# Attention and mixture-of-experts kernel: places of their own for the copies out of PSUM, LayerNorm factors on GpSimd, a mean-free Wo, and one maximum over two PSUM banks

## The chip, the cores and the metric

The kernel is written by hand in Bass and runs on one core of a Trainium2 chip. The metric is the device time of one execution in microseconds; lower is better. The five engines of the core run their own instruction lists in order and meet through semaphores: PE (TensorE), DVE (VectorE), ACT (ScalarE), POOL (GpSimd) and SP (SyncE, which here only issues transfers).

## The reference

Two sandwich blocks over 8 sequences of 256 tokens with 256 features. The first is grouped-query attention with 32 query heads and 8 key heads of size 8, the second a mixture of experts with two shared experts.

```
x = x + layernorm(attn(layernorm(x)) @ Wo + b_out)
x = x + layernorm(moe(layernorm(x)))
attn: q, k rotated by position; softmax(q k / sqrt(8)), causal; times v
moe:  scores = sigmoid(x @ w_router); the two best of 8 experts, weights normalised
      each expert: wd (silu(wg x) * (wu x)), inner size 640
      plus two shared experts of the same form for every token
layernorm(y) = (y - mean(y)) / sqrt(var(y) + 1e-5), no learned factors
```

## The kernel before

The 2048 tokens are 16 tiles of 128 rows. One function, `plan()`, writes a single list of stages, and each engine walks through the list and emits its own part of each stage, so the list is the order of every engine. The attention goes in 64 passes: pass n is one key head of one sequence (8 passes for each of the 8 sequences, two tiles each). `plan()` calls `step(n)` for each pass, and `step` goes through the string `ORDER`, whose letters are places within a step: `2` is `pass2` (scores in banks 0 to 2, `exp` on ACT, the causal mask on POOL), `a` and `b` are `early` and `late` (the scores of pass n+7 in other banks, of which DVE takes the row maxima; `tops` adds the last part of an early bank from within `pass2`), `w` is `weigh` (probabilities times values, two passes later), `v` is `back` (transposing the result, after which DVE divides), `m0` to `m3` are the four parts of `neg` (which splits the negated maxima of four passes into three bf16 terms), and `t` is `turn` (PE transposes them, ACT copies them into `NMT`, SP sends them with six transfers into rows 48 to 50 of the queries `QT`, where the next group's `pass2` needs them).

`s0` to `s3` are the four places of a step in which the work on the tiles stands: the tables `FRONT` and `BACK` give each stage a time in quarter steps, relative to the tile's sequence. The front of a tile is its first LayerNorm (`f_stats`, `f_dev`, `f_norm`), a transpose, the q, k, v product, the rotation with a three-way bf16 split of q and k (`f_rope`, `f_first`, `f_second`, `f_third`) and their transposes (`q0`, `q1`, `k`). The back is the product with Wo (`b_out`), its LayerNorm (`b_stats`, `b_dev`, `b_norm`), the sum with x (`b_add`), the second LayerNorm (`b_stats2`, `b_dev2`, `b_norm2`), a transpose into `XH` and `XL` (the fp32 value as a rounded part and a rest) and the router product (`b_route`).

In all of these one stage means the PE work and at the same place in the list the copy out of PSUM. Four PSUM banks, 3 to 6, go round among all stages but `pass2` and `weigh`, in turn, by `banks()`.

After pass 63 come 155 chunks c of expert work (`up`, `hh`, `hl`, `down`): 20 for the first shared expert, 115 for 23 blocks of 256 rows that the router chose, and 20 for the other shared expert. The backs of the last tiles are mixed into the first chunks, with two steps in each of chunks 0 to 13. The routing (`pick`, `rank`, `choose`, `token`) runs beside chunks 4 to 18; `xt` transposes the gathered rows of a block, and chunk 20 is the first that needs them. The weights of an expert are split into `WH` and `WL` by `split`.

Of the kernel before, what the change touches and what calls it, by code (L numbers as in the profile page):

```python
# [13 lines left out]
P = 128  # L14
# [22 lines left out]
FRONT = [("f_stats", -101), ("f_dev", -97), ("f_norm", -90), ("f_turn", -85), ("f_qkv", -77), ("f_rope", -77),  # L37
         ("f_first", -69), ("f_second", -67), ("f_third", -65), ("q0", -53), ("q1", -56), ("k", -49)]
BACK = [("b_turn", 47), ("b_out", 51), ("b_stats", 51), ("b_dev", 51), ("b_norm", 56), ("b_add", 59),
        ("b_stats2", 59), ("b_dev2", 59), ("b_norm2", 66), ("b_turn2", 71), ("b_route", 75)]  # L40
ORDER = "a 2 s0 d s1 b s2 v m0 t w m1 m2 m3 s3"
# [14 lines left out]
def plan():  # L56
# [5 lines left out]
    halves, turns, pairs = [], [], []  # L62

    def sides(n):
        for b in range(NB):
            for stages, lag in ((FRONT, LAG), (BACK, 16)):
                for what, at in stages:
                    for T in range(2):
                        if n == max(32 * b + at + lag * T, 4 * START):
                            out.append((what, 2 * b + T))  # L70

    def step(n):
        firsts = ahead.get(n, [])
        for o in ORDER.split():
            if o == "2" and 0 <= n < 64:
                out.append(("pass2", n))
            if o == "a":
# [24 lines left out]
            if o == "t":  # L102
                out.extend(("turn", m) for m in turns)
                turns.clear()
            if o[0] == "s":
                sides(4 * n + int(o[1]))

    for n in range(START, JOIN):
        step(n)
        if n == 0:  # L110
            out.append(("router_split", 0))
# [3 lines left out]
    for c in range(NC + 4):  # L115
        if c < 14:
            for n in (JOIN + 2 * c, JOIN + 2 * c + 1):
# [19 lines left out]
        if c == DENSE - 1:  # L137
# [1202 lines left out]
```

## Time and profile before

| | us |
|---|---|
| median of 3 runs | 758.98 (756.83 to 760.82) |
| the profiled execution | 760.28, span 757.8 from the first to the last instruction |
| PE busy | 705.5 (93%) |
| DVE busy | 605.7 (80%) |
| ACT busy | 431.8 (57%) |
| POOL busy | 314.7 (42%) |

The span has three parts: the attention, up to about 298 us; the first shared expert with the routing beside it, up to about 402 us; and the routed blocks and the second shared expert. A busy share is an average over all of them, so each part is read by itself. The ends of matmuls are modelled in such a profile, and a PE that is shown busy is not PE at its peak.

### The profile page before, as it was taken

What the parts mean: (1) busy time and instruction counts of PE and PEld (TensorE: products, weight loads), DVE (VectorE), ACT (ScalarE), POOL (GpSimd) and SP (SyncE); (2) the same over time, 40 slices, a digit from 0 to 9 for tenths busy, and PEclk for the clock granted to TensorE, in tenths of its full rate; (3) what the DMA queues carried; (4) which work ended last, traced back from release to release, by engine and by line L of the source; (5) the groups of instructions that cost most, each with busy time, mean ns of one, the idle gap of its engine ahead of it and who ended that gap; (6) DMA issues with size and microseconds to landing.
All of it is one profiled execution on the core that took longest, in us unless ns stands there. A gap on an engine that the chain in (4) does not pass through costs nothing. (4 is left out here: it accounts for less than half of the span.)

```text
span 757.8 us, 15818 instructions
## 1 busy us (share of the span) xinstructions
PE 705.5 (93%) x6002; PEld 564.7 (75%) x6002; DVE 605.7 (80%) x1364; ACT 431.8 (57%) x729; POOL 314.7 (42%) x444
## 2 busy tenths in 40 slices
PE   4779999999999998979998999999999999999994
PEld 2335555555555555768888999999999999988884
DVE  4998999999998885565866888888878878738885
ACT  2436765666667576334244777777776777632230
POOL 4113354454444455100223455445445543048854
PEclk9989999999999999989999999999999999999998
DMA  8000000000000000000124676776667676513311
GB/s 278 1 3 4 4 3 10 16 10 11 10 11 10 16 11 15 15 8 1 43 91 174 208 236 217 223 236 216 239 217 233 221 215 202 163 56 90 91 57 55
DMA packets 29131, 74.31 MB, mean 98 GB/s; under 512 B 4609, under 2 KB 18305, under 8 KB 29057
## 3 DMA queue, kind: packets, MB, share of 16 engines
q0 software_dynamic: 12208, 55.45, 22.6%
q1 hardware_dynamic: 16432, 17.20, 6.9%
q8 instruction: 48, 0.79, 0.4%
q10 hardware_dynamic: 416, 0.66, 0.3%
q14 instruction: 27, 0.21, 0.1%
HBM read 62.68 MB, written 10.22 MB: 96 GB/s over the span
## 5 line engine op out<-in xcount | busy, mean ns | idle before, releaser
L984 DVE TENSOR_TENSOR HF<-SS,PS 128x256 f32<-128x256 f32 (+1 forms) x155 | 75.9, 490 | 98.2 <-ACT SS L732 57.0
L732 ACT ACTIVATE SS<-PS 128x256 f32<-128x256 f32 (+1 forms) x155 | 68.2, 440 | 116.7 <-PE PS L396 112.2
L396 PE MATMUL PS<-XGH,WH 128*128 128x256 f32 x460 | 129.6, 282 | 2.8 <-DVE WL L1084 2.8
L396 PE MATMUL PS<-XGL,WH 128*128 128x256 f32 x460 | 129.3, 281 | 0.0
L396 PE MATMUL PS<-XGH,WL 128*128 128x256 f32 x460 | 129.3, 281 | 0.0
L821 DVE TENSOR_REDUCE NM<-PS 128x2 f32<-128x512 f32 (+1 forms) x192 | 122.6, 682 | 7.6 <-PE PS L396 6.6
L1084 DVE TENSOR_TENSOR WL<-RAW,WH 128x768 fp32r<-128x768 f32 x125 | 120.2, 963 | 3.5 <-ACT WH L659 2.8
L396 PE MATMUL PS<-WH,HH 128*128 128x256 f32 x390 | 112.4, 288 | 0.9 <-DVE ACC L995 0.8
L659 ACT ACTIVATE HH<-HF 128x256 fp32r<-128x256 f32 (+1 forms) x155 | 72.1, 465 | 71.4 <-DVE HF L984 64.1
L396 PE MATMUL PS<-WL,HH 128*128 128x256 f32 x390 | 110.4, 283 | 0.0
L396 PE MATMUL PS<-WH,HL 128*128 128x256 f32 x390 | 110.4, 283 | 0.0
L694 ACT ACTIVATE PF<-PS 128x1536 f32<-128x1536 f32 x64 | 92.9, 1451 | 27.4 <-PE PS L396 27.4
L1180 POOL TENSOR_SCALAR_AFFINE_SELECT PF<-PF 128x512 f32<-128x512 f32 x128 | 80.6, 654 | 62.9 <-ACT PF L694 62.9
L659 ACT ACTIVATE WH<-RAW 128x768 fp32r<-128x768 f32 x125 | 104.5, 838 | 1.0 <-DMA RAW<-in_wb,WIDX 0.7
L396 PEld LDWEIGHTS PS<-XGH,WH 128*128 128x128 f32 x460 | 86.7, 189 | 3.0 <-DVE WL L1084 3.0
L396 PEld LDWEIGHTS PS<-XGH,WL 128*128 128x128 f32 x460 | 87.3, 190 | 0.0
L396 PEld LDWEIGHTS PS<-XGL,WH 128*128 128x128 f32 x460 | 87.0, 189 | 0.0
L396 PEld LDWEIGHTS PS<-WH,HH 128*128 128x128 f32 x390 | 74.2, 190 | 3.3 <-issue 1.5
L1094 DVE TENSOR_TENSOR HL<-HF,HH 128x256 fp32r<-128x256 f32 (+1 forms) x155 | 76.4, 493 | 0.1
L396 PEld LDWEIGHTS PS<-WL,HH 128*128 128x128 f32 x390 | 74.5, 191 | 1.6
L1145 POOL TENSOR_SCALAR VE<-MV 128x1 f32<-128x1 f32 x64 | 19.0, 297 | 134.0 <-DVE MV L1020 46.8
L396 PEld LDWEIGHTS PS<-WH,HL 128*128 128x128 f32 x390 | 74.2, 190 | 0.0
(167 smaller groups left out, 1460.2 us busy)
## 6 DMA issues: line engine op xcount, KB each, us to landing
ys<-YO SPq DMA_DIRECT2D x23, 256.0 KB
RAW<-in_wsh SPq DMA_DIRECT2D x4, 768.0 KB, 6.5
X<-in_x SPq DMA_DIRECT2D x8, 256.0 KB, 5.3
xn<-YY SPq DMA_DIRECT2D x16, 128.0 KB, 1.7
out<-X SPq DMA_DIRECT2D x16, 128.0 KB
QT<-NMT SPq DMA_DIRECT2D x96, 4.0 KB
RAW<-in_wsh SPq DMA_DIRECT2D x2, 384.0 KB, 6.1
XG<-xn,XIDX POOLq DMA_INDIRECT x46
```

Source lines behind the costliest of these rows:

```text
L396: return eng.matmul(o, l, r, start=start, stop=stop, skip_group_check=True)
L659: return eng.activation(o, i, ACT.Copy)
L694: eng.activation(PF[:, i % 3, :], PS[:, 0:1536], ACT.Exp, scale=SCALE).then_inc(expd, 1)
L732: t = eng.activation(SS[:, i % 2, 0:n], bank(b, 0, n), ACT.Silu)
L821: eng.tensor_reduce(o, i, AXX, ALU.max, negate=True).then_inc(free[c], 1)
L984: eng.tensor_tensor(HF[:, c % 2, 0:n], SS[:, c % 2, 0:n], bank(b, 512 - n, 512) if n == 256 else bank(b), ALU.mult).then_inc(free[b], 1)
L1084: eng.tensor_tensor(WL[q % 2][:, c], RAW[:, c], WH[q % 2][:, c].bitcast(F32), ALU.subtract).then_inc(w_lo, 1)
L1094: eng.tensor_tensor(HL[:, i % 4, 0:n], HF[:, i % 2, 0:n], HH[:, i % 4, 0:n].bitcast(F32), ALU.subtract).then_inc(h_lo, 1)
L1145: eng.tensor_scalar(VE[:, i:i + 1], MV[:, i, 1:2], EPS, None, ALU.add, ALU.bypass).then_inc(ve, 1)
L1180: eng.affine_select(out=o, in_=o, pattern=[[0, 4], [1, 128]], base=0, channel_multiplier=-1, compare_op=ALU.is_ge, fill=0.0).then_inc(zero ...
```

## The change

Six things change.

1. Each copy out of PSUM becomes a stage of its own (`f_turned`, `f_taken`, `q0_out`, `b_taken`, `b_high`, `b_kept`, `divide`, `weighed`, `turned`, `exp`, and so on) with a place of its own in `ORDER` or in the tables. All tables get new numbers, with own tables for the first two sequences. `banks()` takes the bank that was used longest ago instead of strict turns.
2. The two maxima of a `late` pair are one DVE instruction over two neighbouring banks (`maxima`), and DVE frees both banks together.
3. `f_norm` and `b_norm2` move from DVE to POOL.
4. Wo and b_out have their row means subtracted at the start (`prepare`, on DVE in steps 1 to 6), so that the product has mean zero: `b_norm` is gone, and `b_add` multiplies by the factor and adds x in one instruction. The bias goes into PSUM through one more bf16 matmul, and ACT copies the sum out (`b_taken`) where DVE added the bias.
5. The router product takes both parts of its weights at once: 4 matmuls of 16 columns for 8 of 8, and DVE adds the two halves for all tiles (`pick` 0).
6. The copies of k in `KC` come out of wider casts: DVE has 4 instructions for 6 there.

```diff
-ORDER = "a 2 s0 d s1 b s2 v m0 t w m1 m2 m3 s3"
+ORDER = "a 2 b s0 d x l s1 m0 s2 v V w t T W m1 m3 s3 m2"
+RANK, TOKEN, ROWS0 = 11, 18, 19.0
...
+                    mm(bank(c, 0, 256), ones3[:, :], B3[:, :], True, False)
                     for k in range(2):
-                        t = mm(bank(c, 0, 256), CTT[:, i % 2, 128 * k:128 * k + 128], WO[:, k, :], k == 0, k == 1)
+                        t = mm(bank(c, 0, 256), CTT[:, i % 2, 128 * k:128 * k + 128], WO[:, k, :], False, k == 1)
...
-                        for a, r in ((XH, WRH), (XH, WRL), (XL, WRH), (XL, WRL)):
-                            t = mm(bank(c, 0, 8), a[:, k, 128 * i:128 * i + 128], r[:, 8 * k:8 * k + 8], n == 0, n == 7)
+                        for a in (XH, XL):
+                            t = mm(bank(c, 0, 16), a[:, k, 128 * i:128 * i + 128], WRX[:, k, :, :].rearrange("p a e -> p (a e)"),
+                                   k == 0 and a is XH, k == 1 and a is XL)
...
+                elif what == "b_taken":
+                    made(e, ("b_out", i))
+                    made(e, ("b_turn2", i - 2))
+                    e.wait_ge(d_xn[i % 2], 16 * (i // 2))
+                    copy(YY[:, i % 2, :], bank(c, 0, 256)).then_inc(free[c], 1)
...
-                eng.tensor_copy(K[:, :, 0:4:3, :], R[:, 32:40, :].unsqueeze(2).broadcast_to([P, 8, 2, 8]))
-                eng.tensor_copy(K[:, :, 5, :], R[:, 32:40, :]).then_inc(k_1, 1)
+                eng.tensor_copy(K[:, :, :, 1:6:2, :], R[:, 32:40, :].unsqueeze(2).unsqueeze(3).broadcast_to([P, 8, 2, 3, 8])).then_inc(k_1, 1)
...
-                eng.tensor_copy(KC[:, T, :, 1, :], KC[:, T, :, 0, :]).then_inc(k_5, 1)
...
+                    c = lates[k][0]
+                    e.wait_ge(laid, 2 * k + 2)
+                    eng.tensor_reduce(o.rearrange("p (j a) -> p a j", a=2), bank(c, 0, 1024).rearrange("p (a j t) -> p a j t", a=2, j=2),
+                                      AXX, ALU.max, negate=True).then_inc(n_m, 1)
...
+            def prepare(k):
+                if k < 3:
+                    e.wait_ge(d_bo if k == 2 else d_wo, 16)
+                    src = BO if k == 2 else WO[:, k, :]
+                    eng.bn_stats(BN[:, 48 + k, :], src[:, :]).then_inc(wo_s, 1)
...
-                    eng.tensor_tensor(YY[:, i % 2, :], bank(c, 0, 256), BO[:, :], ALU.add).then_inc(free[c], 1)
...
-                    normed(YY[:, i % 2, :], YY[:, i % 2, :], 16 + i).then_inc(b_yn, 1)
...
-                    eng.tensor_tensor(X1[:, i, :], X1[:, i, :], YY[:, i % 2, :], ALU.add).then_inc(b_x1, 1)
+                    e.wait_ge(b_rs, i + 1)
+                    eng.scalar_tensor_tensor(out=X1[:, i, :], in0=YY[:, i % 2, :], scalar=RS[:, 16 + i:17 + i], in1=X1[:, i, :],
+                                             op0=ALU.mult, op1=ALU.add).then_inc(b_x1, 1)
...
+                elif what == "b_norm2":
+                    e.wait_ge(c_rs, i + 1)
+                    made(e, ("b_turn2", i - 2))
+                    eng.tensor_scalar(YY[:, i % 2, :], X1[:, i, :], MV[:, 32 + i, 0:1], RS[:, 32 + i:33 + i],
+                                      ALU.subtract, ALU.mult).then_inc(c_x2, 1)
```

How the order moves, at three places. The first is DVE in the middle of the attention, where `b_out`, `b_stats` and `b_dev` of a tile meet the four parts of `neg`. `NM`, `NBF` and `NR` are the maxima and their bf16 terms, `BN` and `MV` the statistics, `YY` the product with Wo, `RA` and `RB` parts of the rotation. Before:

```order
L763 TENSOR_SCALAR YY<-X,MV,RS 128x256 [waits c_rs]
L850 RECIPROCAL RC<-PS 128x16 [waits free4,full4]
L853 TENSOR_TENSOR CTX<-PS,RC 128x2x64 [waits sums]
L833 CAST NBF<-NM 128x4x8 [waits free5,free6,free4,free3]
L836 TENSOR_TENSOR NR<-NM,NBF 128x32 [waits n_0]
L839 CAST NBF<-NR 128x4x8 [waits n_1]
L842 TENSOR_TENSOR NBF<-NR,NBF 128x4x8 [waits n_2]
L1047 TENSOR_TENSOR YY<-PS,BO 128x256 [waits d_xn1,full5]
L1050 BN_STATS BN<-YY 128x6 [waits free5]
L1053 BN_AGGR MV<-BN 128x2 [waits b_st]
```

And of the change:

```order
L892 CAST NBF<-NR 128x4x8 [waits n_1]
L827 TENSOR_TENSOR RA<-RQ,ROPE 128x320 [waits free6]
L828 TENSOR_TENSOR RB<-RQ,ROPE 128x40x4
L829 TENSOR_TENSOR RB<-RQ,ROPE 128x40x4
L870 TENSOR_REDUCE NM<-PS 128x4 [waits full4]
L874 TENSOR_REDUCE NM<-PS 128x2x2 [waits laid]
L1123 BN_STATS BN<-YY 128x6 [waits free3]
L895 TENSOR_TENSOR NBF<-NR,NBF 128x4x8 [waits n_2]
L1126 BN_AGGR MV<-BN 128x2 [waits b_st]
L1140 TENSOR_TENSOR XL<-PS,XH 128x2x128 [waits c_xh]
```

Two DVE instructions on `YY` are gone, steps that wait for each other no longer follow each other directly, and the last part of `neg` stands one step later.

The second place is ACT between the copy of `turn` into `NMT` and the `exp` of the first pass that needs it. `PF` is the output of an `exp`, one for each pass. Before, from the row behind the copy:

```order
L659 ACTIVATE NMT<-PS 48x256 [waits d_nm3,d_nm2,d_nm4,d_nm1,d_nm5,d_nm0,full6]
L659 ACTIVATE YC<-PS 128x256 [waits pv]
L659 ACTIVATE XH<-PS 128x2x128 [waits full3]
L694 ACTIVATE PF<-PS 128x1536 [waits scored]
L659 ACTIVATE QT<-PS 128x8x128 [waits full5]
L659 ACTIVATE ES<-PS 128x8 [waits full5]
L659 ACTIVATE QT<-PS 128x8x128 [waits full6]
L659 ACTIVATE XNT<-PS 128x256 [waits full3]
L694 ACTIVATE PF<-PS 128x1536 [waits pv,scored]
L659 ACTIVATE YC<-PS 128x256 [waits full4,pv]
L659 ACTIVATE CTT<-PS 128x256 [waits full3]
L659 ACTIVATE KT<-PS 128x8x128 [waits full4]
```

The row that follows is the `exp` that needs the transfers. Of the change:

```order
L744 ACTIVATE PF<-PS 128x1536 [waits scored]
L707 ACTIVATE QT<-PS 128x8x128 [waits full5]
L707 ACTIVATE NMT<-PS 48x256 [waits d_nm3,d_nm2,d_nm4,d_nm1,d_nm5,d_nm0,full3]
L707 ACTIVATE EW<-PS 128x16 [waits full4]
L707 ACTIVATE XNT<-PS 128x256 [waits full5]
L744 ACTIVATE PF<-PS 128x1536 [waits pv,scored]
L707 ACTIVATE CTT<-PS 128x256 [waits full5]
L707 ACTIVATE YC<-PS 128x256 [waits pv]
L707 ACTIVATE KT<-PS 128x8x128 [waits full6]
L744 ACTIVATE PF<-PS 128x1536 [waits scored]
```

One whole `exp` lies between the copy and the one that needs it, where there were two.

The third place is DVE at chunks 18 to 20, where the routed blocks begin. `XGL` is the rest part of the first block's rows, `WL` that of its weights. Before:

```order
L1084 TENSOR_TENSOR WL<-RAW,WH 128x768 [waits w_hi] x2
L968 TENSOR_REDUCE WAB<-EQ 128x16 [waits rt]
L969 TENSOR_TENSOR CMB<-CMB,EQ 128x128
L971 TENSOR_REDUCE WAB<-CMB 128x16 [waits rt]
L984 TENSOR_TENSOR HF<-SS,PS 128x512 [waits h_lo,full3,free2]
L1094 TENSOR_TENSOR HL<-HF,HH 128x512 [waits h_hi]
L1084 TENSOR_TENSOR WL<-RAW,WH 128x768 [waits w_hi] x3
L1098 TENSOR_TENSOR XGL<-PS,XGH 128x512 [waits x_hi]
```

And of the change:

```order
L1148 TENSOR_TENSOR WL<-RAW,WH 128x768 [waits w_hi] x2
L1052 TENSOR_REDUCE WAB<-EQ 128x16 [waits rt]
L1053 TENSOR_TENSOR CMB<-CMB,EQ 128x128
L1055 TENSOR_REDUCE WAB<-CMB 128x16 [waits rt]
L1162 TENSOR_TENSOR XGL<-PS,XGH 128x512 [waits x_hi]
L1068 TENSOR_TENSOR HF<-SS,PS 128x512 [waits h_lo,full3,free2]
L1158 TENSOR_TENSOR HL<-HF,HH 128x512 [waits h_hi]
L1148 TENSOR_TENSOR WL<-RAW,WH 128x768 [waits w_hi] x3
```

`XGL` moved ahead of chunk 19's work and of the three weight splits. `token` stands one chunk later on PE (before `up` 18 instead of before `up` 17), and `xt` 0 one chunk earlier (before `up` 19).

## Rows read from the trace of the kernel before

**Rows 1.** Busy time by stretch: from:to length, PE, PEld, DVE, ACT, POOL, clock, DMA.

```profile
60.00:80.00 20.00, 19.62 (x230) 10.90 (x224) 18.37 (x51) 14.60 (x18) 7.17 (x14) 0.97 0.02 4
154.49:188.84 34.35, 32.73 (x355) 19.24 (x354) 33.07 (x93) 22.51 (x31) 16.24 (x30) 1.00 0.04 11
320.00:340.00 20.00, 16.05 (x86) 13.84 (x84) 11.21 (x21) 7.00 (x11) 1.58 (x4) 0.83 0.02 7
```

**Rows 2.** Timeline of ACT: the exp of passes 15, 42 and 63.

```profile
106.19 1.46 ACT L694 ACTIVATE PF<-PS 128x1536 f32<-128x1536 f32 x1
...
222.93 1.45 ACT L694 ACTIVATE PF<-PS 128x1536 f32<-128x1536 f32 x1 [0.68 <-PE PS L396]
...
293.68 1.45 ACT L694 ACTIVATE PF<-PS 128x1536 f32<-128x1536 f32 x1 [0.37 <-PE PS L396]
```

**Rows 3.** Waits of DVE from 120 to 240: us in total, times, longest.

```profile
DVE NM L821 <- PE PS L396: 1.0, 3, 0.4
```

**Rows 4.** DVE by line and shape, 154.4 to 188.8: busy us, mean ns.

```profile
L821 DVE TENSOR_REDUCE NM<-PS 128x2 f32<-128x512 f32 x16 | 10.3, 684 | 0.2
...
L763 DVE TENSOR_SCALAR YY<-X,MV,RS 128x256 f32<-128x256 f32 x2 | 1.2, 610 | 0.0
...
L785 DVE CAST QC<-RR 128x768 bf16<-128x768 f32 x2 | 1.1, 560 | 0.1
...
L1047 DVE TENSOR_TENSOR YY<-PS,BO 128x256 f32<-128x256 f32 x2 | 0.8, 418 | 0.0
...
L763 DVE TENSOR_SCALAR YY<-YY,MV,RS 128x256 f32<-128x256 f32 x2 | 0.8, 408 | 0.0
L763 DVE TENSOR_SCALAR XN<-X,MV,RS 128x256 f32<-128x256 f32 x2 | 0.8, 404 | 0.0
...
L808 DVE COPY KC<-KC 128x512 bf16<-128x512 bf16 x2 | 0.6, 296 | 0.1
...
L790 DVE CAST KC<-RR 128x128 bf16<-128x128 f32 x2 | 0.4, 218 | 0.0
```

**Rows 5.** DVE by line, 322 to 345: a maximum over 896 elements.

```profile
L881 DVE TENSOR_REDUCE SG<-RK 128x112 f32<-128x896 f32 x1 | 1.1, 1086 | 0.0
```

**Rows 6.** Single lines, ns min/median/max: multiply-add on DVE; on POOL, 256 and 512 elements.

```profile
L1010 DVE SCALAR_TENSOR_TENSOR ACC<-YG,WAB,ACC x32: 472/485/2145, 680.8 to 736.9; 128x256 f32<-128x256 f32 x32
L1221 POOL TENSOR_TENSOR X<-X,ACC x15: 716/745/1276, 698.4 to 753.3; 128x256 f32<-128x256 f32 x15
L1180 POOL TENSOR_SCALAR_AFFINE_SELECT PF<-PF x122: 627/637/1354, 51.6 to 289.0; 128x512 f32<-128x512 f32 x122
```

**Rows 7.** Timeline of PE and SP at one turn; the page's landing time of a transfer.

```profile
151.49 0.29 PE L606 MATMUL PS<-CB,NBF 128*48 128x128 bf16 x2
...
152.41 4.03 SPq L1255 DMA_DIRECT2D QT<-NMT  x6
...
xn<-YY SPq DMA_DIRECT2D x16, 128.0 KB, 1.7
```

**Rows 8.** Timeline of PE around the second transpose of tile 15.

```profile
332.78 0.69 PE L406 MATMUL PS<-CF,YY 128*128 128x128 f32 x2 [3.94 <-DVE YY L763]
333.12 0.78 PE L396 MATMUL PS<-XH,WH 128*128 128x512 f32 x1
...
337.54 0.46 PE L396 MATMUL PS<-XL,WH 128*128 128x512 f32 x1
```

**Rows 9.** Timeline of DVE and POOL where the first block's rows come.

```profile
390.22 0.25 DVE L963 COPY IDS<-PS 128x92 f32<-128x92 f32 x1
...
401.29 0.68 DVE L1098 TENSOR_TENSOR XGL<-PS,XGH 128x512 fp32r<-128x512 f32 x1
...
392.24 0.95 POOL L1163 DMA_INDIRECT XG<-xn,XIDX  x1 [0.30 <-issue]
```

**Rows 10.** Waits of PE from 286 to 412; the chain that ended last, its first PE piece.

```profile
PE PS L396 <- DVE WL L1084: 2.8, 1, 2.8
...
402.07 8.52 PE PS L396 x57
```

More of the change, by code:

```diff
@@ L76, in step @@
                 out.append(("pass2", n))
+            if o == "x" and 0 <= n < 64:
+                out.append(("exp", n))
             if o == "a":
@@ L109, in plan @@
         step(n)
-        if n == 0:
-            out.append(("router_split", 0))
+        if 1 <= n < 8:
+            out.append(("prepare", n - 1))
         if EARLY <= n < EARLY + 5:
@@ L115, in plan @@
     for c in range(NC + 4):
-        if c < 14:
-            for n in (JOIN + 2 * c, JOIN + 2 * c + 1):
+        if c < len(TAILS):
+            first = JOIN + sum(TAILS[:c])
+            for n in range(first, first + TAILS[c] if c < len(TAILS) - 1 else JOIN + 28):
                 step(n)
@@ L353, in build @@
         stages = plan()
-        use = banks(stages)
+        use, after, lates = banks(stages)
         def wide(mask, k):
@@ L400, in take @@
                 e.wait_ge(free[b], k - 1)
+                e.wait_ge(n_m, after.get(key, 0))
                 return b
@@ L460, in late @@
             def late(k):
-                cs = [take(("late", k, a)) for a in range(2)]
+                c, f0, f1, m = lates[k]
+                cs = (c, c + 1)
+                e.wait_ge(free[c], f0)
+                e.wait_ge(free[c + 1], f1)
+                e.wait_ge(n_m, m)
                 for a in range(2):
@@ L690, in _ @@
                     copy(NMT[:, i % 2, :], bank(c, 0, 128).bitcast(BF16)[0:48, :]).then_inc(free[c], 1)
-                elif what == "pass2":
+                elif what == "exp":
                     e.wait_ge(scored, 2 * i + 2)
@@ L750, in _ @@
                     copy(YO[:, q % 2, :, :].rearrange("p q d -> p (q d)"), bank(b)).then_inc(free[b], 1)
-                elif what == "pick" and s[2] == 0:
+                elif what == "pick" and s[2] == 1:
                     t0, n = PICKS[i]
-                    for t in range(t0, t0 + n):
-                        read(e, ("b_route", t))
+                    e.wait_ge(picked[i], 1)
                     es = ES[:, t0:t0 + n, :].rearrange("p t e -> p (t e)")
@@ L829, in neg @@
                         read(e, ("early", 4 * m + k))
-                        for a in range(2):
-                            read(e, ("late", 4 * m + k, a))
+                    e.wait_ge(n_m, 4 * m + 4)
                     made(e, ("turn", m - 1))
@@ L1084, in _ @@
                     eng.tensor_tensor(WL[q % 2][:, c], RAW[:, c], WH[q % 2][:, c].bitcast(F32), ALU.subtract).then_inc(w_lo, 1)
-                elif what == "pick" and s[2]:
+                elif what == "pick" and s[2] != 1:
                     pick(i, s[2])
@@ L1184, in _ @@
                 what, i = s[0], s[1]
-                if what == "pass2":
+                if what == "exp":
                     causal(i)
@@ L1249, in _ @@
                 what, i = s[0], s[1]
-                if what == "turn":
+                if what == "turned":
                     b, h = i // 2, i % 2
-                    read(e, s)
+                    read(e, ("turn", i))
                     for a in range(2):
@@ L1256, in _ @@
                                           NMT[24 * a + 8 * r:24 * a + 8 * r + 8, i % 2, :]).then_inc(d_nm[3 * a + r], 16)
+                elif what == "prepare" and i == 4:
+                    e.wait_ge(wo_c, 7)
+                    for r in range(3):
+                        eng.dma_start(B3[r:r + 1, :], BB[:, r, :]).then_inc(d_b3, 16)
                 elif what == "b_norm2":
```

280 lines of the change are left out of this document (162 added, 118 removed).

## The prediction

> **What bounds the kernel now.** I read the busy times by stretch first, then the waits, then the chain. In the middle of the attention the pattern repeats every 8 passes, and 154.49 to 188.84 is one such period of 34.35 us: DVE 33.07 busy, PE 32.73, ACT 22.5, POOL 16.2 [rows 1]. Two engines look full. The waits tell them apart: over the 120 us around it, the largest wait of DVE for PE sums to 1.0 us [rows 3]. DVE always has its next instruction at hand, so DVE is the bound there, and PE, whose ends are modelled, waits in small pieces. In 60 to 80, before the backs of tiles begin, PE issued 230 matmuls in 20 us (11.5 per us); in the period it issued 355 in 34.35 (10.3 per us) [rows 1]. The kinds are the same but for the mix, so PE has room for something like a tenth more.
>
> The whole stage has one clock, the `exp` of each pass: pass 15 at 106.19, pass 42 at 222.93, pass 63 at 293.68 [rows 2]. That is 4.32 us a pass over 27 passes, and (293.68 - 222.93)/21 = 3.37 over the last 21, as first the fronts and then the early and late stages run out.
>
> Behind the attention PE is the bound. The chain that ended last begins in earnest at 402.07 with matmuls and hardly leaves PE [rows 10]; nothing of the change touches that part. Between 298 and 402 PE is stopped in two places that the change does touch: 3.94 us before the second transpose of tile 15 [rows 8], and 2.8 us before the first routed block [rows 10]. After either stop the matmuls run slower for some us: the granted clock over 320 to 340 is 0.83, so part of it at 1.2 instead of 2.4 GHz [rows 1].
>
> The profiled execution took 760.28, with a span of 757.8, and is 1.3 above the median of 758.98. I make the sum against 760.28 and take off 1.3 at the end.
>
> **The middle of the attention.** What leaves DVE in 8 passes (two tiles) [rows 4]: XN<-X 0.8, YY<-X 1.2, YY<-YY 0.8, YY<-PS 0.8, together 3.6. The maxima: 16 instructions in 10.3 us become 8 over 1024 elements. One of 512 takes 0.684 and one of 896 takes 1.086 [rows 4, 5], that is 1.05 ns an element, so one of 1024 takes 1.22, and eight 9.7 less some overlap of neighbours, 9.4: saved 0.9. So the joint maximum saves only a start each time, since the elements stay. K: KC<-KC (0.6) goes, and the casts of 128 and 64 elements become one of 384; by the slope of 560 ns at 768 and 218 at 128 that is 0.355, and two later ones double their elements. In all 0.3 saved. `b_add` becomes a multiply-add: its shape takes at least 0.472 [rows 6] against some 0.41 for a plain add, 0.1 more. Sum 4.7, so 33.07 becomes 28.4 busy. To it comes the 1.3 that DVE was not busy in the period; the parts of `neg` and of the statistics no longer wait for each other directly, which gives back up to a half of it. DVE then needs about 29.2 for 8 passes, 3.65 a pass.
>
> PE: 8 router matmuls fewer per period and 2 bias matmuls more, 349 of them. At the 11.5 per us of 60 to 80 that is 30.4 us, 3.80 a pass. If instead its busy time is taken at its word, 32.73 less six at its mean of 0.092, it is 32.1, some 4.00 a pass. ACT's period holds eight `exp` of 1.45 [rows 2] and 23 others, so these take (22.51 - 11.6)/23 = 0.47 each; two more make 23.4 of 30, and ACT is no bound. POOL gets four instructions of 256 elements. The trace has none of that kind on POOL; a two-input one of that shape takes 0.745 and a one-input one of 512 elements 0.637 [rows 6], so 0.4 to 0.75 each. I take 0.5: 2 us on 16.2 of 30. What covers this is POOL's idle half; with it gone, the mask and then `weigh` would be late.
>
> I take 3.80 a pass, PE just ahead of DVE as the bound: 27 passes times (4.32 - 3.80) = **14.0 us**, with 3.65 (18.1) and 4.00 (8.6) as bounds.
>
> **The rest of the attention.** Before pass 12 no back runs. DVE is at 18.4 of 20 there, and saves in 8 passes only the maxima, XN and K (2.0), 3 us up to pass 12. `prepare` adds 15 instructions in steps 1 to 6: ten of 256 columns at 0.41 and five short ones at up to 0.22 [rows 4], 5.2 us. Its cover is what DVE gains there and some idle tenths. I set the stretch to **0**, from -3 to +2. After pass 42 fronts fade, the backs still save; the last passes are held by the `exp` itself, 1.45 each, and the scores between. I take **4 us** for 21 passes, 0.2 a pass, from 1 to 8.
>
> **Tile 15's chain.** Before, DVE had the first three long parts of the routing between the statistics of tile 15 and its factor. Now only one short addition stands there (`pick` 0), `b_norm` is gone, and its second factor is applied by POOL, idle there. That takes more than 3 us out of DVE's part and POOL adds at most 0.3, so the 3.94 goes nearly whole. With it goes the slow clock behind it: the matmuls from 333.12 to 337.54 [rows 8] take 4.4 us, and twice the clock would halve that, 2.2 us. Four routers on PE's path here give 16 matmuls less 4 for the bias, 12 at 0.092, about 1. **7 us**, from 3 to 8.
>
> **The first routed block.** PE waited 2.8 us there, the wait is put down to WL, but the last thing to come was XGL at 401.29, behind three splits of weights [rows 9]. The change puts it ahead of them, a chunk earlier. What is late next is the gather itself: from IDS at 390.22 the second gather is issued by 393.19 [rows 9] and, with the 1.7 of a stored transfer [rows 7] as nearest row for a landing, there at 394.9, 4.7 us. PE's cover between `token` and `xt` is `up` 18 and `down` 16, 24 matmuls; at 16.05 us for 86, the mean of 320 to 340 [rows 1], 4.5. So a new stop of some 0.2, at most 0.7, against 2.8, and the slow clock behind it, again about 2. **4 us**, from 1 to 5.
>
> **Sum.** 14.0 + 0 + 4 + 7 + 4 = 29. 760.3 - 29 = 731.3, and less 1.3: **730**. Ends of all terms together: gain of 10.6 and of 41, so 748 and 718.
>
> **A rule against it.** YY<-X on DVE takes 610 ns, the same operation as YY<-YY 408 [rows 4]. Both read and write 256 columns of SBUF, so something else holds the first, and a mask of POOL at the same time is the nearest explanation. The Trainium skill (SBUF — State Buffer, Who interferes with whom) says why: a DVE instruction with two SBUF inputs or in a two-port mode shares its second port pair with GpSimd, and whoever comes first holds it. By that rule, the trace agrees: 610 against 408. And GPSIMD Engine Reference, Engine selection, would keep elementwise work on VectorE, as GpSimd is about 2x slower with two inputs and near line rate with one. By the first rule each new POOL instruction can block DVE for its own time.
>
> **Rivals.**
> - *DVE pays for POOL's new work.* 32 new POOL instructions of 0.5; if each held DVE for 0.5 in full, a period would get 4 x 0.5 = 2 back, 31.2 for DVE, 3.90 a pass, and the middle 11.3: 733 to 735. Against: the blocked one among the old instructions leaves DVE too. Inside the range; chance 0.10.
> - *PE really is full* (4.00 a pass, gain in the last part of the attention 2): 8.6 + 2 + 11 = 21.6, less 2 for `prepare`: 739. For: 32.73 of 34.35. Chance 0.20.
> - *Everything fits*: 3.65 a pass, tails at their best: 18.1 + 6 + 13 + 1 = 38, 721. Chance 0.15.
> - *The six transfers come late*, and this ends on the other side. From the transpose of `turn` (151.49) to the end of the last issue (152.41 + 4.03 = 156.44) 4.95 us pass, and a 1.7 landing that starts with the last of six issues, at 155.77, ends at 157.5: 6.0 us [rows 7]. Before, PE had two and three quarters passes for that, 11.9 us at 4.32. Now `turn` stands a step later, with one whole `exp` between: about 1.25 passes, 4.8 us at 3.8. So every fourth pass PE can stop for 1.2 us, behind it all of `pass2`, the maxima DVE waits for, and the `exp`. Where PE has other small waits this is the same time; if it comes on top, 16 x 1.2 = 19 us, and the gain shrinks to 10: 748. It decides against the change if the stop passes 2 us (16 x 2 = 32): a cover down to 4.0, or transfers that take 6.8, would do. Result 762 to 765. Chance 0.08 for that, 0.12 for 742 to 755.
> - *The change does not do what it says*: the orders are tied up in other waits (a `late` pair needs two free neighbours of four banks and holds both for 1.2 us), passes stay at 4.2, and only the two tails are gained: 3 + 11 - 3 = 11, 748. Chance 0.08.
>
> **How the numbers follow.** My own forecast (724 to 737) has 0.27, DVE paying 0.10, PE full 0.20, everything fits 0.15, the milder late transfers 0.12, tied orders 0.08, the severe ones 0.08. A measurement of this kernel can tell about 0.5% (3.8 us) from no change. Only the severe case and a part of the tied orders reach beyond 755: faster 0.87, same 0.05, slower 0.08. The range leaves out the severe case, half of the milder one above 748 and the best tail: 718 to 748, and with the 2 us by which the shown runs stray from their median, 716 to 750.
>
> **What would show it.** In the middle, `exp` 15 to 42 in 27 x 3.8 = 103 us; DVE with waits for PE of more than 1 us in 120; the joint maximum at 1.22; POOL's tensor_scalar of 256 at 0.4 to 0.75. No wait of 3.9 before tile 15's transpose and none of 2.8 before chunk 20; the third part of the span unchanged at some 356 us. A wait of PE for transfers into QT would show the late ones. Wrong I would be if a wait in every fourth pass is larger than 2 us, or if POOL's instructions take 1 us and delay the mask.

## The result, and the profile after

The changed kernel takes 778.53 us (median of 4 runs, 776.7 to 778.75) against 759.38 for the kernel before: 1.025 times as long, with an interval of 1.022 to 1.028. The forecast was 730, with 716 to 750 as range. The profiled execution took 778.75, with a span of 776.8.

The three parts of the span show where to look. The attention ends 31 us later, and of that the stretch behind it gives 12 back. Busy time by stretch, with the columns of [rows 1]: first 60 to 80, then passes 15 to 42.

```profile
60.00:80.00 20.00, 16.87 (x181) 8.99 (x184) 18.23 (x44) 12.72 (x14) 10.33 (x15) 0.91 0.01 2
117.20:240.66 123.46, 112.52 (x1166) 63.82 (x1164) 101.71 (x244) 79.28 (x108) 69.17 (x114) 0.97 0.03 10
```

The timeline of ACT, with the exp of passes 15, 42 and 63, to be laid beside [rows 2]:

```profile
117.20 1.45 ACT L744 ACTIVATE PF<-PS 128x1536 f32<-128x1536 f32 x1 [0.41 <-PE PS L438]
...
240.66 1.45 ACT L744 ACTIVATE PF<-PS 128x1536 f32<-128x1536 f32 x1
...
324.37 1.45 ACT L744 ACTIVATE PF<-PS 128x1536 f32<-128x1536 f32 x1 [0.37 <-PE PS L438]
```

A pass takes 123.46/27 = 4.57 us in the middle, where it took 4.32, although DVE's work fell as intended: 101.71 us busy in 27 passes, where the same view of the kernel before has 111.98. No engine is full now. So something waits, and the waits of PE over the whole span name it at the top (us in total, times, longest):

```profile
PE PS L438 <- DMA QT<-NMT: 30.6, 16, 3.9
PE PS L449 <- POOL XN L1264: 10.6, 2, 8.8
```

That is 16 waits for the 16 groups of four passes. The kernel before has no such row. One of them in PE's timeline, with SP's row beside it:

```profile
207.59 0.29 PE L653 MATMUL PS<-CB,NBF 128*48 128x128 bf16 x2
...
212.05 0.39 PE L438 MATMUL PS<-CB 128*128 128x512 bf16 x1
213.76 0.39 PE L438 MATMUL PS<-QT,KT 64*128 64x256 bf16 x2 [1.32 <-DMA QT<-NMT]
...
208.32 4.05 SPq L1330 DMA_DIRECT2D QT<-NMT  x6
```

`turn` starts at 207.59, PE has work until 212.44, 4.85 us later, and the last transfer is there at 213.52 (in the chain below 211.74 + 1.78), after 5.93. The chain that ended last shows what these 5.9 us are, one thing behind the other: the transpose, ACT's copy, SP's issues (the first of six is shown, the others follow it) and the landing of the last transfer:

```profile
207.66 0.24 PE PS L653 x2
...
207.92 0.39 ACT NMT L707
...
208.32 0.65 SPq L1330
...
211.74 1.78 DMA QT<-NMT
...
213.76 1.29 PE PS L438 x10
```

Such a stop costs more than its own length where the clock falls behind it. The granted clock falls to half, 1.2 instead of 2.4 GHz, ten times between 50 and 325 us, each time in or shortly behind one of the 16 stops. It does not fall behind each: in passes 15 to 42 that is two stops of seven. The four us from one us behind the stop that ended at 157.02, and behind the one of the timeline above:

```profile
158.00:162.00 4.00, 4.00 (x19) 2.02 (x22) 2.59 (x4) 1.62 (x2) 2.31 (x3) 0.57 0.12 37
214.80:218.80 4.00, 4.00 (x38) 2.12 (x37) 3.76 (x11) 1.78 (x3) 2.90 (x5) 1.00 0.10 33
```

PE is full in both, but gets 19 matmuls done in the first and 38 in the second. Over the whole span, SP's issues have 7% of the chain that ended last and the transfers another 4%, where the kernel before had neither:

```profile
PE 78%; SPq 7%; DVE 5%; DMA 5%; ACT 2%; issue 2%; POOL 2%; POOLq 0%; DVEq 0%; ACTq 0%
PE PS L438 72%; SPq L1330 7%; DMA QT<-NMT 4%; PE PS L449 2%; PE PS L541 2%; PE PS L623 1%; DVE NM L874 1%; ACT NMT L707 1%; DVE NM L870 1%; POOL RS L1213 1%; DMA X<-in_x 1%; PE PS L653 0%; ACT QT L707 0%; POOL XN L1264 0%; ACT PF L744 0%
```

Behind the attention the two stops of [rows 8] and [rows 10] are gone. What PE still waits for between 324.4 and 434:

```profile
PE PS L449 <- ACT YC L707: 0.9, 1, 0.9
PE PS L449 <- DVE CTX L906: 0.8, 1, 0.8
PE PS L623 <- DMA XG<-xn,XIDX: 0.6, 1, 0.6
PE PS L449 <- POOL YY L1268: 0.4, 1, 0.4
```

All kernels below in one table. Each entry is a moment in the profiled execution (us from the start): the exp of passes 0, 15, 42 and 63, the SiLU of chunk 12, the first matmul on gathered rows ("first block"), the SiLU of chunk 134, the end of the span. "15 to 42" is the difference of two columns; the last column is the median time of the kernel's executions, for two_transfers_again the time of its only one.

| kernel | exp 0 | exp 15 | exp 42 | 15 to 42 | exp 63 | chunk 12 | first block | chunk 134 | end | median |
|---|---|---|---|---|---|---|---|---|---|---|
| before | 49.2 | 106.19 | 222.93 | 116.74 | 293.7 | 364.2 | 402.1 | 660.0 | 757.8 | 759.4 |
| changed | 52.6 | 117.20 | 240.66 | 123.46 | 324.4 | 387.8 | 422.7 | 678.9 | 776.8 | 778.5 |
| turn_one_step_earlier | 52.2 | 114.31 | 226.54 | 112.23 | 297.2 | 360.5 | 395.5 | 651.6 | 754.0 | 756.6 |
| two_transfers | 50.4 | 106.69 | 216.24 | 109.55 | 284.1 | 347.4 | 382.4 | 638.6 | 745.2 | 746.8 |
| two_transfers_again | 49.7 | 106.00 | 215.58 | 109.58 | 282.6 | 346.0 | 380.9 | 637.2 | 735.9 | 737.6 |
| before_turn_late | 49.9 | 111.47 | 228.84 | 117.37 | 311.6 | 381.5 | 419.3 | 677.2 | 774.9 | 778.2 |
| late_but_two_transfers | 49.9 | 103.64 | 219.16 | 115.52 | 289.7 | 359.6 | 397.5 | 655.4 | 753.9 | 758.5 |
| before_two_transfers | 48.9 | 107.39 | 224.00 | 116.61 | 294.7 | 365.4 | 403.3 | 661.1 | 758.9 | 759.6 |
| two_norms_on_dve | 47.9 | 104.53 | 221.29 | 116.76 | 290.2 | 358.1 | 393.3 | 649.4 | 755.9 | 759.7 |
| two_seed_twice | 50.4 | 107.76 | 221.26 | 113.50 | 292.2 | 355.6 | 391.0 | 647.4 | 746.0 | 748.1 |
| two_no_seed | 51.5 | 107.83 | 215.22 | 107.39 | 283.4 | 346.7 | 381.7 | 637.9 | 735.8 | 735.7 |
| before_seed_twice | 49.1 | 108.27 | 227.02 | 118.75 | 299.7 | 370.7 | 408.6 | 666.6 | 774.9 | 777.3 |
| before_no_seed | 49.6 | 105.86 | 222.16 | 116.30 | 291.4 | 361.0 | 398.9 | 658.1 | 755.8 | 757.3 |
| two_prepare_later | 48.1 | 103.91 | 213.46 | 109.55 | 280.5 | 343.9 | 378.9 | 635.0 | 733.7 | 737.7 |
| two_first_norms_on_dve | 46.4 | 102.65 | 212.20 | 109.55 | 281.4 | 344.8 | 379.8 | 636.0 | 734.7 | 735.5 |
| two_both_starts | 46.5 | 102.25 | 211.83 | 109.58 | 280.3 | 343.7 | 378.7 | 634.9 | 733.6 | 735.5 |
| two_rows_as_before | 49.7 | 106.03 | 215.58 | 109.55 | 285.2 | 348.6 | 386.4 | 645.4 | 743.3 | 742.8 |
| two_picks_as_before | 49.4 | 106.51 | 216.06 | 109.55 | 283.1 | 351.7 | 386.7 | 642.9 | 741.6 | 743.3 |

### The profile page after: what moved, and what is told of

Same layout as the page of the kernel before. It is cut to its first block, busy times and chain, and to the rows that moved or that the text cites. A ratio compares the mean times of both kernels' runs of the same rounds, so it can differ in the third digit from the quotient of the medians.

```text
span 776.8 us, 15538 instructions
## 1 busy us (share of the span) xinstructions
PE 711.8 (92%) x5954; PEld 561.1 (72%) x5954; DVE 584.5 (75%) x1219; ACT 439.2 (57%) x745; POOL 353.5 (46%) x477
## 4 chain that ended last, share of the span: by engine, by line
PE 78%; SPq 7%; DVE 5%; DMA 5%; ACT 2%; issue 2%; POOL 2%; POOLq 0%; DVEq 0%; ACTq 0%
PE PS L438 72%; SPq L1330 7%; DMA QT<-NMT 4%; PE PS L449 2%; PE PS L541 2%; PE PS L623 1%; DVE NM L874 1%; ACT NMT L707 1%; DVE NM L870 1%; POOL RS L1213 1%; DMA X<-in_x 1%; PE PS L653 0%; ACT QT L707 0%; POOL XN L1264 0%; ACT PF L744 0%
## 5 line engine op out<-in xcount | busy, mean ns | idle before, releaser
L1246 POOL TENSOR_SCALAR_AFFINE_SELECT PF<-PF 128x512 f32<-128x512 f32 x128 | 78.6, 639 | 107.5 <-ACT PF L744 106.8
L874 DVE TENSOR_REDUCE NM<-PS 128x4 f32<-128x1024 f32 x64 | 78.0, 1218 | 2.4 <-PE PS L438 2.4
L870 DVE TENSOR_REDUCE NM<-PS 128x4 f32<-128x512 f32 x64 | 43.9, 686 | 36.8 <-PE PS L438 36.6
```

Of the source, the lines that this page charges most:

```text
L870: eng.tensor_reduce(o, bank(c).rearrange("p (h t) -> p h t", t=128), AXX, ALU.max, negate=True).then_inc(free[c], 1)
L874: eng.tensor_reduce(o.rearrange("p (j a) -> p a j", a=2), bank(c, 0, 1024).rearrange("p (a j t) -> p a j t", a=2, j=2), AXX, ALU.max, nega ...
L1246: eng.affine_select(out=o, in_=o, pattern=[[0, 4], [1, 128]], base=0, channel_multiplier=-1, compare_op=ALU.is_ge, fill=0.0).then_inc(zero ...
```

## Experiments on the late transfers

**turn_one_step_earlier.** Only the place of the last part of `neg` changes, and with it the step of `turn`:

```diff
-ORDER = "a 2 b s0 d x l s1 m0 s2 v V w t T W m1 m3 s3 m2"
+ORDER = "a 2 b s0 d x l s1 m0 s2 v V m3 w t T W m1 s3 m2"
```

> The changed kernel with the last part of `neg`, and so `turn`, one step earlier. In the changed kernel PE waits for the transfers into QT 16 times, 30.6 us in all, and the granted clock of the attention is lower. Late transfers as the cause: cover grows from about 1.25 to 2.25 passes (9 us against 6.0), these waits go to under 3 us, and the time falls from 778.5 by 30 for the waits and up to 8 for the clock, to 740 to 750; passes 15 to 42 come down from 4.57 to 3.9 to 4.1 us each. Rival, the orders are tied up elsewhere (banks, pairs of late, POOL): PE waits as long for something else, and the time stays above 770.

756.58 us (ratio to before 0.994, 0.991 to 0.998): 22 us less than the changed kernel, but not the 740 to 750 that I expected. The waits for QT fall to one, of 2.0 us. A wait of another kind has come, since the last part of `neg` now stands just ahead of the transpose:

```profile
PE PS L653 <- DVE NBF L895: 10.5, 7, 2.6
```

Behind chunk 134 this profile has 4.6 us more than the kernel before; the last section comes back to that.

**two_transfers.** The order is untouched. The transfers become two; the rest of the edit only counts two semaphores where there were six:

```diff
-                        for r in range(3):
-                            eng.dma_start(QT[64 * a + 48 + r:64 * a + 49 + r, b % 3, 8 * h:8 * h + 8, :],
-                                          NMT[24 * a + 8 * r:24 * a + 8 * r + 8, i % 2, :]).then_inc(d_nm[3 * a + r], 16)
+                        eng.dma_start(QT[64 * a + 48:64 * a + 51, b % 3, 8 * h:8 * h + 8, :],
+                                      NMT[24 * a:24 * a + 24, i % 2, :]).then_inc(d_nm[a], 16)
```

> The changed kernel with the order untouched, but the maxima of a group go into QT in two transfers of 24 partitions instead of six of 8, so that the time from the transpose to the last landing falls from 5.9 to some 3.3 us (four issues of 0.68 fewer). Late transfers as the cause: with a cover of 4 to 5 us the waits of PE for them nearly vanish, time 740 to 752, as with an earlier transpose, though not one instruction of an engine moved. Rival, orders tied up elsewhere: above 770.

746.83 us (ratio 0.982, 0.978 to 0.987). SP issues for 1.47 us instead of 4.05. From the start of the second issue to the landing the trace shows 2.2 us, once, at the last turn, where PE waited for it; with that the rows are there some 3.7 us after `turn` starts (an estimate from 185.93, the start of this turn, and 187.4, that of the second issue), not 5.9. One wait for QT is left in the whole span, at the last turn, where only 2.8 us of work cover the transfers:

```profile
186.66 1.47 SPq L1329 DMA_DIRECT2D QT<-NMT  x2
...
PE PS L438 <- DMA QT<-NMT: 1.5, 1, 1.5
```

Passes 15 to 42 go from 123.46 to 109.55. Of the 13.9 us, 10.2 are the seven waits, and the other 3.7 go with the clock, 0.97 before and 1.00 now: two falls to half of it are gone with the stops.

**before_turn_late.** The other way round: only this step of the change, put into the kernel before.

```diff
-ORDER = "a 2 s0 d s1 b s2 v m0 t w m1 m2 m3 s3"
+ORDER = "a 2 s0 d s1 b s2 v m0 w t m3 m1 m2 s3"
```

> The kernel before, with nothing but the last part of `neg` and `turn` moved so that the transpose stands behind the weighing two steps later, as in the changed kernel. Late transfers as the cause: PE waits for QT at each of 16 turns, 0.5 to 1 us in the middle, where passes are 4.3 us, and 1.5 to 3 in passes 0 to 12 and after 42; time 770 to 785, so that this alone makes the kernel before as slow as the changed one. Rival, the other parts of the change cost the time: within 4 us of 759.

778.19 us (ratio 1.025, 1.023 to 1.027), as slow as the changed kernel, by this alone:

```profile
PE PS L396 <- DMA QT<-NMT: 22.3, 16, 3.5
```

Where it costs is telling: 0.6 us in passes 15 to 42, 5.3 up to pass 15 and 12.0 behind pass 42, where passes are short. In the middle there are seven stops too, 5.0 us in all, but each is only 0.6 to 1.1 long, the clock stays at 1.00, and DVE is the bound there, so nearly all of it is room that PE had.

**before_two_transfers** and **late_but_two_transfers** are the controls: the shorter issue in the kernel before, and in the one with the late transpose.

> The kernel before with two transfers for six. Its transpose has 2.75 passes of cover, so late transfers as the cause expects no gain: within 3 us of 759. If six issues cost the kernel something else (a queue, ports of SBUF), it is faster by more than 4 us, and then the shorter latency in the changed kernel would not be a clean test.

> The kernel before with the late transpose (which took 778.2) and two transfers for six. Late transfers as the cause: with 3.3 us of latency against a cover of 4 to 5 the waits for QT go, and the time comes back to 759, at most 764. Rival: moving `neg` and `turn` costs by the changed order of DVE and PE itself; then it stays above 770.

759.6 (ratio 1.000, 0.999 to 1.001) and 758.47 (0.997, 0.995 to 0.999). Six issues cost nothing where the transpose is early, and the late transpose costs nothing where the issues are few. Only both together cost some 19 us. With that the cause of the slower kernel is shown from both sides.

## Experiments on the terms that were left

**Which engine bounds the middle.** The matmul of 512 columns that lays the mask into the bank of `early` was issued twice, or left out; without it the row maxima of the first halves are taken over masked scores too.

```diff
                 mm(bank(c).rearrange("p (a t) -> p a t", a=4), ident, wide(maskn, 4), True, False)
+                mm(bank(c).rearrange("p (a t) -> p a t", a=4), ident, wide(maskn, 4), True, False)
```

> The changed kernel with two transfers, and in every pass the matmul of 512 columns that lays the mask into the bank of `early` is issued twice (the second overwrites the first with the same). It is 0.22 us more for PE and nothing for the other engines. PE full as the bound: passes 15 to 42 go from 109.55 by 27 x 0.22 = 5.9 to 115, the total up by 10 to 14, to 757 to 761. If something else bounds them, PE hides it: within 2 us in these passes.

> The kernel before with the same doubled matmul. DVE as the bound of its middle: passes 15 to 42 stay within 2 us of 116.7, and the total rises by 2 to 6 only, where DVE isn't the bound (passes 0 to 12, after 42). If PE is the bound there too: 116.7 becomes 122 to 123, and the total 770 or more.

> The changed kernel with two transfers, without the matmul of 512 columns that lays the mask into the bank of `early` (the row maxima of the first halves are then taken over masked scores too): 0.22 us less for PE in each pass. If PE alone bounds passes 15 to 42 they fall from 109.55 by 5.9 to 103.6; if DVE, at 101.5 busy and with its waits, is right behind it, by 1 to 4 only.

> The kernel before without the same matmul. DVE as the bound of its middle: passes 15 to 42 stay at 116.7, at least 115.5. If PE's share is as large as the doubled one showed (a third), they fall by 2 to 114.7.

Passes 15 to 42 of two_transfers, two_seed_twice, two_no_seed, and then of before_seed_twice and before_no_seed, in the columns of [rows 1]:

```profile
106.69:216.24 109.55, 108.81 (x1166) 62.33 (x1164) 101.49 (x244) 79.29 (x108) 68.91 (x114) 1.00 0.04 12
107.76:221.26 113.50, 113.43 (x1191) 63.38 (x1189) 101.83 (x242) 79.79 (x107) 68.90 (x114) 1.00 0.04 11
107.83:215.22 107.39, 103.41 (x1141) 59.73 (x1141) 102.78 (x244) 79.26 (x108) 68.58 (x114) 1.00 0.04 12
...
108.27:227.02 118.75, 114.99 (x1202) 65.51 (x1201) 112.16 (x311) 75.92 (x101) 54.81 (x101) 1.00 0.04 11
105.86:222.16 116.30, 105.34 (x1146) 62.80 (x1146) 112.15 (x309) 75.67 (x101) 54.93 (x101) 0.99 0.04 11
```

I had set the step at 27 x 0.22 = 5.9 us of PE; by PE's busy time it is 4.3 to 5.4 (108.81 to 113.43 and to 103.41; 109.66 in the kernel before, to 114.99 and to 105.34). In the kernel before, taking it away gives 0.4 and adding it costs 2.0: DVE bounds it, and PE has some 3 to 4 us of room in 116.7, three per cent. With two transfers, taking it away gives 2.2 and adding it costs 3.95: PE bounds it, and DVE is 2 us behind. The totals of these four are not to be compared, for the reason given under the last heading: before_seed_twice took 777.3, where I expected 2 to 6 us more than before, but up to chunk 134 it is only 6.5 us late, and the rest comes behind that.

**two_norms_on_dve.** `f_norm` and `b_norm2` moved from the list of POOL into that of DVE, at the same places of the plan.

> The changed kernel with two transfers (746.8), and `f_norm` and `b_norm2` back on DVE at the same places of the list. PE full as the bound of the middle: DVE gets 4 x 0.41 a period, 101.5 becomes 107 of 109.55 for passes 15 to 42, and these still take 109 to 111; the total within 3 us of 747. Rival, POOL's new work holds DVE up: taking it away gives time back, passes 15 to 42 below 107 and the total below 742. Rival, DVE is still the bound: passes 15 to 42 at 114 or more.

759.67 us, and passes 15 to 42 in 116.76: the number of the third of my expectations, but not its reason, since DVE is not full, at 104.26 of 116.76. The windows, DVE's largest wait, and the two instructions that came (busy us, mean ns):

```profile
104.53:221.29 116.76, 110.18 (x1166) 61.77 (x1164) 104.26 (x257) 79.21 (x107) 53.49 (x101) 1.00 0.03 11
...
DVE YY L1134 <- POOL RS L1222: 7.0, 7, 1.0
...
L1134 DVE TENSOR_SCALAR YY<-X,MV,RS 128x256 f32<-128x256 f32 x7 | 6.1, 875 | 7.0 <-POOL RS L1222 7.0
...
L1130 DVE TENSOR_SCALAR XN<-X,MV,RS 128x256 f32<-128x256 f32 x6 | 2.3, 389 | 0.0
```

DVE becomes busier by 2.8 us, though the 13 instructions that came are busy for 8.4: the other 5.6 went elsewhere. Most of that are two short instructions of `neg`, L892 and L889, that POOL's causal mask held up in two_transfers, with means of 547 and 402 ns over the same passes, and that have 182 each here. In their place the mask now holds up L1134, 875 where the instruction has about 410 by itself. So what DVE loses to POOL is lost to the mask, an old instruction, and depends on what stands beside it. And the factor comes from POOL, so DVE now waits for it, seven times 1.0 us. 2.8 and 7.0, less 2.6 us of other idle time, make the 7.2. At these places of the plan the move to POOL pays by the wait that DVE hasn't; whether `b_norm2` on DVE at a later place would cost anything was not tried.

**two_prepare_later, two_first_norms_on_dve, two_both_starts.**

```diff
-        if 1 <= n < 8:
-            out.append(("prepare", n - 1))
+        if 7 <= n < 14:
+            out.append(("prepare", n - 7))
```

and `f_norm` of tiles 0 to 3 in DVE's list, with the same instruction.

> The changed kernel with two transfers (first exp at 50.39, pass 12 at 94.33, pass 15 at 106.69), and `prepare` in steps 7 to 13 instead of 1 to 7. If the 5.2 us of `prepare` hold up DVE at the start, exp 0 comes at about 49.3 (it does not hold up what stands before step 1), pass 7 some 3 to 5 us earlier, and pass 12 to 15 get part of it back: pass 15 at 104 to 106. If idle tenths cover it, pass 15 stays within 0.5 of 106.69.

> The changed kernel with two transfers, and `f_norm` of the first four tiles only back on DVE. PE waits 10.6 us for POOL's XN there (9.6 for DVE's in the kernel before), and with all norms on DVE exp 0 came at 47.88 instead of 50.39. If the first tiles' norm on POOL costs the start its time: exp 0 at 48 to 48.5 and pass 12 to 42 all some 2 us earlier, passes 15 to 42 unchanged at 109.5. Rival: the start waits for x to load and gets nothing, exp 0 within 0.5 of 50.4.

> The changed kernel with two transfers, `prepare` in steps 7 to 13 and the first four `f_norm` on DVE. Apart, pass 15 came 2.8 and 4.0 us earlier. If both shorten the same start one after the other, pass 15 comes at 100 to 101 and the total is 732 to 734; if each only filled the gap that the other leaves, pass 15 at 102.5 and the total 735 to 736.

737.73 (ratio 0.972, 0.969 to 0.975), 735.53 (0.969, 0.966 to 0.972) and 735.47 (0.969, 0.966 to 0.972). Against two_transfers, pass 15 comes 2.8 and 4.0 us earlier, with both 4.4 (the repetition of two_transfers, further down, has it 0.7 earlier by itself): they shorten the same stretch, and the second of my expectations holds. The last two are 24 us under the kernel before, with two_no_seed (735.7) the fastest of the whole study.

**two_rows_as_before and two_picks_as_before.** Each takes one step of the stretch behind the attention back.

```diff
-RANK, TOKEN, ROWS0 = 11, 18, 19.0
+RANK, TOKEN, ROWS0 = 11, 17, 19.5
```

```diff
-PICK = {4: [(0, 0)], 5: [(0, 1), (0, 2), (0, 3)], 6: [(0, 4)], 7: [(0, 5), (0, 6)], 8: [(0, 7), (0, 8), (1, 0), (1, 1), (1, 2),
-        (1, 3), (1, 4), (1, 5), (1, 6), (1, 7), (1, 8)], 9: [(0, 9), (1, 9)]}
+PICK = {4: [(0, k) for k in range(5)], 5: [(0, 5), (0, 6)], 6: [(0, 7), (0, 8)], 7: [(0, 9)],
+        8: [(1, k) for k in range(10)]}
```

> The changed kernel with two transfers, and `token` again before up 17 and `xt` 0 again behind hh 19. By my step on the first routed block the stop of some 2.8 us and the low clock behind it come back: from the exp of pass 63 to the first matmul on gathered rows 101 to 102.5 us instead of 98.3. If the place of these two is worth nothing, within 0.7 of 98.3.

> The changed kernel with two transfers, and the parts of the routing back in the chunks of before (five parts of `pick` in chunk 4). By my step on the chain of tile 15 DVE is then late with that tile's second LayerNorm: a wait of 2.5 to 4 us of PE before its transpose, low clock behind it, and from the exp of pass 63 to the SiLU of chunk 12 some 5 to 7 us more than the 63.3 of two transfers (70.5 in the kernel before). If the freed norms already shortened the chain enough, under 2 us.

From exp 63 to the first block 101.2 us against 98.3, and from exp 63 to chunk 12 68.6 against 63.4. The waits are back, each in its kernel:

```profile
PE PS L438 <- DVE WL L1148: 2.8, 1, 2.8
```

```profile
PE PS L449 <- POOL YY L1268: 4.0, 2, 3.6
```

**two_transfers_again.** The same kernel once more, on another chip, in a single execution.

> The changed kernel with two transfers once more. If the stop in the second shared expert belongs to the kernel, the stretch from the SiLU of chunk 134 to the end is 105 to 108 us again; if it belongs to the execution, it may be the 97.8 of the kernels before and after, and the execution takes 737 to 739.

737.63 us: up to chunk 134 the two profiled executions agree to 1.4 us, and from there to the end one takes 106.6 and the other 98.7.

## Why the prediction was wrong

**The step that failed** is the rival *The six transfers come late*. Its numbers were right: "6.0 us" of latency were measured as 5.93, "4.8 us" of cover as 4.85, a stop of "1.2 us" as 1.32 in the group shown. Wrong was what I made of them: "Where PE has other small waits this is the same time", and with it a chance of 0.20 for a cause whose every term stood in my own sum. There were no other waits to hide in, since PE was to be the bound. I also priced all groups with the cover of the middle. The chain takes 5.9 us at twelve of the 16 turns and 6.2 to 6.8 at the others; the cover is 4.85 in the middle, but 3.7 to 4.7 before pass 15 and down to 2.7 behind pass 42, where passes are shorter, and stops reach 3.9 us: 30.6 in all where I had 19. The low clock behind ten of the stops was not in the term at all, although I had counted it behind the two stops of [rows 8] and [rows 10]. Up to chunk 134 the changed kernel is 40.3 us behind two_transfers and 41.7 behind its repetition. 28 to 29 of that are the waits, and the 11 to 14 left go with the clock: 0.92, 0.97 and 0.90 in the three parts of the attention, where two_transfers has 1.00, 1.00 and 0.97.

The severe form of the rival, 762 to 765, falls short too. It stands on the 730 of the forecast, and without the stops the kernel would gain 20 us and not 29, as worked out below: 759 - 20 + 40 = 779, and 778.5 was measured.

The stops also add up: PE's own order holds `turn`, so each stop puts off the next `turn` as well, and nothing later catches it up.

**The middle: 14 predicted, 7.2 without the stops** (116.74 to 109.55). The bound "PE really is full", 4.00 a pass, was the right one: 4.06. I had taken PE's speed from 60 to 80, where the mix of matmuls is another, and got a tenth of room; there was a third of that. DVE too fell by less: its busy time in 27 passes by 10.5 us where 4.7 a period make 15.9. The 5.4 are about what the mask holds up: L892 and L889 by 4.1 us, and the multiply-add, that I set at 0.472 and that has a median of 666 ns, by 1.6 in the middle. Another size was wrong without showing in DVE: POOL's instruction that I set at 0.5, with 0.4 and 0.75 as bounds, takes 1240. That was one of the two things by which I said I would be wrong. The mask does start some 1.2 us late in every fourth pass of two_transfers, but PE has no wait for it.

```profile
L1129 DVE SCALAR_TENSOR_TENSOR X<-YY,RS,X x16: 473/666/923, 115.9 to 354.5; 128x256 f32<-128x256 f32 x16
L1264 POOL TENSOR_SCALAR XN<-X,MV,RS x16: 1224/1240/1807, 7.6 to 222.9; 128x256 f32<-128x256 f32 x16
```

**DVE pays for POOL's new work** did not come: in passes 15 to 42 of two_transfers no DVE instruction is longer while one of the 13 new POOL instructions runs, where the rival had 6.8 us (2 a period). What DVE pays there, 5.7 us beyond the shortest times of its instructions, it pays to the mask, and the kernel before pays 2.4 the same way. Only in turn_one_step_earlier does a new one, `b_norm2`, hold up a cast, by 1.4 us in all. Which instruction meets the mask is a matter of the order: L892 has 181 ns in the changed kernel, and in two_transfers, where it falls on the mask, a median of 523 for 180 at best:

```profile
L892 DVE CAST NBF<-NR x16: 180/523/549, 40.0 to 268.9; 128x32 bf16<-128x32 f32 x16
...
194.82 0.55 DVE L892 CAST NBF<-NR 128x32 bf16<-128x32 f32 x1
...
194.10 1.23 POOL L1246 TENSOR_SCALAR_AFFINE_SELECT PF<-PF 128x512 f32<-128x512 f32 x2
```

The cast starts behind the mask and ends with it, at 195.37 and 195.33. The Trainium skill (SBUF — State Buffer, Who interferes with whom) has a DVE cast or tensor_scalar in its two-port mode and a GpSimd instruction shut each other out. By that rule, the trace agrees.

**The rest of the attention.** From the start to pass 15 I had 0; without the stops it is -0.5 (two_transfers) and +0.2 (its repetition), and in it `prepare` and the first norms on POOL hold 4.4 that a better place gives back. Behind pass 42 I had 4, measured 2.9 and 3.7 (70.75 to 67.82 and 67.01).

**Tile 15's chain**: 7 predicted, 7.2 measured (exp 63 to chunk 12: 70.55 to 63.38). Taking the place of the picks back costs 5.2 of it, so that much is the place; that the rest is the shorter chain was not tried by itself. **The first routed block**: 4 predicted, 2.9 measured (chunk 12 to the first block: 37.84 to 34.95), and by its own experiment 2.9. The new stop for the gather is 0.6, within the 0.7 that I allowed. The third part of the changed kernel is 354.1 us long, where I expected 356.

Without the late transfers the sum is 7.2 - 0.5 + 2.9 + 7.2 + 2.9 = 20 us of gain against 29 forecast. The terms behind the attention were nearly right, the middle was half.

## What to carry to other kernels

Where data take a detour over another engine's copy and a queue of transfers, add up that chain from the trace (here 0.33 + 0.40 for the transpose and the copy, five issues of 0.68 ahead of the last, and 1.78 for its landing, 5.9 us) and compare it with the work that the waiting engine has in between, in each stage of the kernel and with the shorter passes that the change is to bring. If the chain is longer, the stop comes once for every turn of the loop, with a low clock behind some of these stops (here ten of 16), and that is the forecast, not a rival.

How many issues such a chain holds matters more than the bytes: two transfers of the same bytes instead of six took some 2.2 us out of it. An engine's room is read by adding a known small piece of work and taking it away, not from its busy share or from the rate of another stage.

## What the runs showed of the hardware

- A transfer of 4 KB from 8 partitions into 1 lands 1.78 us after its issue begins (2.0 in two of the 16 groups), one of 12 KB from 24 into 3 after 2.2, and SP needs 0.64 and 0.70 us for the issue: three times the bytes over three times the partitions cost 0.4 us more. The Trainium skill (SBUF — State Buffer, The DMA setup-cost knee) has a roughly fixed 2 us a transfer that doesn't scale with bytes. By that rule, the trace agrees nearly: 1.78 and 2.2.
- POOL takes 1240 ns for a subtract-multiply of 256 columns (1200 from its start to that of the next instruction behind it), DVE 404 for the same [rows 4]. The Trainium skill (GPSIMD Engine Reference, Engine selection) has one-input work on GpSimd at roughly line rate. That doesn't hold here, it is three times as long; the measurement decides.
- A stop of PE is not always followed by a low clock: in passes 15 to 42 of the changed kernel seven stops of 1.3 to 2.0 us had two falls behind them, and in those of before_turn_late seven stops of 0.6 to 1.1 us had none.
- Some executions stop for 5 to 10 us in the second shared expert, while POOL issues the gathers of `YG`. From chunk 134 to the end, two_transfers and its repetition:

```profile
638.60:745.20 106.60, 89.89 (x498) 77.28 (x496) 67.75 (x141) 26.35 (x44) 58.69 (x79) 0.94 0.20 62
```

```profile
637.20:735.90 98.70, 87.58 (x498) 75.63 (x496) 67.84 (x141) 26.04 (x44) 59.05 (x79) 0.97 0.22 67
```

  In the first, ACT stands for 8.52 us with a releaser that the trace doesn't find:

```profile
674.00 0.60 ACT L787 ACTIVATE SS<-PS 128x512 f32<-128x512 f32 x1 [8.52 <-remote]
```

  The text of the kernel alone doesn't bring it, since the same kernel has it and hasn't it. turn_one_step_earlier (102.4 from chunk 134), two_norms_on_dve (106.5) and before_seed_twice (108.3) have it in their profiles; the kernel before (97.8) and the changed one (97.9) don't. Whether it comes with the single execution, the chip or the way a program lies in memory is not told apart: the repetition ran on another chip, all four profiles with the stop come from two chips, which gave four without it too, and the ten times of two_norms_on_dve lie close together, at 757.9 to 761.3. The profiled times of these kernels are 5 to 10 us too long for what their edits do, their medians by an amount that no trace shows, and the table by stages is the measure. The cause stays open.
